# Two graph convolutions: 72 of 104 edge groups gathered from DRAM and 32 read from the table on the chip, in place of 59 and 45

## The reference, cut to what matters

```
msgs = embedding_weight[row] * norm[:, None]          # layer 1
out  = jax.ops.segment_sum(msgs, col, num_segments=n)

h    = features * norm_src[:, None]                   # layer 2
agg  = jax.ops.segment_sum(h[src], dst, num_segments=N_NODES) * norm_dst[:, None]
out  = relu(agg @ weight + bias)
```

## Time and profile before

| | us |
|---|---|
| median of 3 runs (lowest, highest) | 7875.66 (7863.07, 7904.74) |
| the profiled execution's own time | 7890.42 |
| its span | 7888.7 |
| PE busy in the span | 6027.0 (76%) |
| DVE busy | 3734.3 (47%) |
| POOL busy | 3873.9 (49%) |
| ACT busy | 1754.8 (22%) |
| L900, reading the table, PE busy | 1120.3 |
| L398, gathers of the convolutions, POOL busy | 458.7 and 443.0 (two groups of buffers) |

### The profile page before, as it was taken

How to read it: one execution, slowest core, us unless ns; L and a number is a source line. 1 busy time by engine, 2 the same in 40 slices (tenths; PEclk the granted TensorE clock), 3 DMA queues, 4 the chain that set the end, 5 groups by cost and what they waited for, 6 DMA issues and landing times.

```text
span 7888.7 us, 136475 instructions
## 1 busy us (share of the span) xinstructions
PE 6027.0 (76%) x46669; PEld 3955.1 (50%) x46669; DVE 3734.3 (47%) x7123; ACT 1754.8 (22%) x3748; POOL 3873.9 (49%) x4028
## 2 busy tenths in 40 slices
PE   5888887666666777677788886778878857778787
PEld 4666665566655666534444443344444424444444
DVE  5444443555564555534444445444444544444446
ACT  2222222333330000022222221222222222222221
POOL 4555553444435455355555542555555345555551
PEclk8888886777886777788888887888888879888888
DMA  4444442222212222233333332333333323333332
GB/s 102 129 129 131 128 128 85 53 56 56 57 49 63 62 62 59 57 74 90 88 91 91 91 86 57 84 89 90 88 88 92 87 54 89 88 90 89 93 87 64
DMA packets 689768, 660.52 MB, mean 84 GB/s; under 512 B 398899, under 2 KB 481274, under 8 KB 689082
## 3 DMA queue, kind: packets, MB, share of 16 engines
q1 hardware_dynamic: 555754, 484.41, 20.5%
q0 software_dynamic: 128960, 166.69, 11.1%
q10 hardware_dynamic: 4368, 0.70, 0.1%
HBM read 562.14 MB, written 89.17 MB: 83 GB/s over the span
## 4 chain that ended last, share of the span: by engine, by line
PE 49%; issue 20%; another core or an unknown queue 18%; DVE 7%; ACT 3%; DVEq 2%; DMA 0%; ACTq 0%; POOL 0%; SPq 0%; POOLq 0%
PE ps L1055 14%; PE ps L900 12%; PE ps L994 6%; PE ps L915 2%; PE ps L855 2%; PE ps L1005 2%; PE ps L1015 2%; PE ps L980 1%; PE ps L864 1%; PE ps L974 1%; DVE region L1778 1%; DVE acc L1803 1%; PE ps L842 1%; PE ps L1029 1%
## 5 line engine op out<-in xcount | busy, mean ns | idle before, releaser
L381 POOL DMA_INDIRECT rows<-table,idx x2340 | 2262.4, 967 | 2235.3 <-ACT region L651 1002.6
L1055 PE MATMUL ps<-region,hot 128*128 128x272 f32 x4992 | 1530.4, 458 | 282.6 <-DVE region L1756 149.3
L1055 PEld LDWEIGHTS ps<-region,hot 128*128 128x128 f32 x4992 | 1041.7, 219 | 677.6 <-issue 445.3
L900 PE MATMUL ps<-hot,region 128*128 128x192 bf16 (+1 forms) x8640 | 1120.3, 291 | 322.4 <-issue 291.3
L1803 DVE TENSOR_TENSOR acc<-acc,ps 128x272 f32 x1248 | 545.0, 437 | 1704.9 <-remote 804.5
L662 ACT ACTIVATE region<-ps 128x512 f32<-128x512 f32 x1248 | 677.6, 595 | 2707.6 <-remote 1428.2
L900 PEld LDWEIGHTS ps<-hot,region 128*128 128x128 bf16 x8640 | 911.2, 116 | 467.0 <-issue 391.3
L368 POOL DMA_INDIRECT rows<-table,idx x728 | 700.5, 962 | 530.0 <-PE ps L835 315.8
L994 PE MATMUL ps<-xT,wcat 64*128 64x512 f32 x2496 | 773.6, 697 | 179.3 <-ACT region L662 81.1
L1778 DVE TENSOR_TENSOR region<-ps,region 128x1056 f32<-128x1056 f32 x582 | 725.1, 1252 | 44.5 <-issue 40.9
L398 POOL DMA_INDIRECT rows<-table,idx x480 | 458.7, 956 | 506.6 <-PE ps L927 344.5
(11 more groups left out here) (304 smaller groups left out, 6836.1 us busy)
## 6 DMA issues: line engine op xcount, KB each, us to landing
hot<-hot_dram SPq DMA_DIRECT2D x624, 256.0 KB
turned<-turned_dram SPq DMA_DIRECT2D x624, 128.0 KB
rows<-table,idx POOLq DMA_INDIRECT x3548
hot_dram<-hot SPq DMA_DIRECT2D x104, 512.0 KB
region<-hot_dram SPq DMA_DIRECT2D x90, 512.0 KB
xwin<-table SPq DMA_DIRECT2D x1664, 24.0 KB
region<-d_dram SPq DMA_DIRECT2D x104, 256.0 KB
turned_dram<-turned SPq DMA_DIRECT2D x104, 256.0 KB
```

What stands on the lines that cost most here:

```text
L381: pool.indirect_dma_start(rows[:, n % 2, j, :], None, table, bass.IndirectOffsetOnAxis(ap=idx[:, s:s + 1], axis=0)).then_inc(rows_in3[n % ...
L900: mm = pe.matmul(ps[:, GB + i % 2, 224 * j:224 * j + n], bt[b][:, k, at:at + P], tabparts[:, k::FOLD, (2 + s) * C:(3 + s) * C], start=(k = ...
L1055: mm = pe.matmul(ps[:, sum_bank(k, side, i), 0:PC + H], hot[:, b, 4 * side + 2 * i + j, :], px[b][:, 4 * side + 2 * i + j, :], start=(j == ...
```

## The change

The bound in the rule that splits the groups goes from 9 to 11, and so `PLAIN` has 72 groups, `DENSE` 32 and `ITEMS` 128 dense items with 72 plain groups between them: two dense items and a plain group mostly (56 times), one dense item and a plain group 16 times. Nothing else is edited; all loops follow the lists, in both convolutions.

```
-DENSE = [g for g in range(G) if 7 * g % 16 >= 9]
-PLAIN = [g for g in range(G) if 7 * g % 16 < 9]
+DENSE = [g for g in range(G) if 7 * g % 16 >= 11]
+PLAIN = [g for g in range(G) if 7 * g % 16 < 11]
```

## The result

The changed kernel takes 7795.53 us in the median of four runs (7772.58 to 7798.94), the kernel before 7877.76 in the same session (7863.07 to 7904.74). The ratio is 0.990 with an interval of 0.988 to 0.992: faster by 1%. Predicted were 7821 us and a range of 7690 to 7970.

The account below looks back on a forecast made before the run. No engine is full; a hold on PE during POOL's gather runs sets the round. First convolution -41 us, second -13, together -54: 7890.42 to 7836 profiled, which is 15 above the median, so 7821 us; range 7690 to 7970.

Parts of the forecast that it names:

- The hold: Convolution rounds: from about a run's sixth gather until 1.6 us after its last, PE hardly gets on; signals arrive at 11.6.
- The rival without a hold: Convolutions: a round is its longest engine, POOL's 10.0 us, say 10.2; 7543 us; chance 0.1 together with the instruction-count rival.
- the one by PE's instruction count: Convolutions: PE gets no more than 12.1 to 12.7 instructions a us; -437 us, 7438 us; 0.1 together with the no-hold rival.
- Floor of 11.8 us: Convolution rounds: the plain sum's signal reaches POOL at 11.6 us, POOL starts at 11.8, pausing 1.8 us instead of 5.4.
- All hidden: Rival, both convolutions: everything hides in the hold, rounds of 11.8 us; -46 and -121 us, 7709 us; chance 0.2.
- Second convolution, 12.3 us a round: Second convolution's rounds at 12.3 us, bounds 11.8 and 13.1; 918 us before, 905 after, -13 us.
- the joined pair: With one dense item between plain groups (16 of 72 times), two gather runs join: 24.3 us for two rounds.
- the slip: Convolution rounds: at the lower clock a reading takes longer, the sum can slide into the hold; 0.5 us added.
- First convolution, 13.0 us a round: First convolution's rounds at 13.0 us, bounds 11.8 and 15.2; 995 us before, 954 after, -41 us.
- an extra of 0.7 us for the degree count: First convolution: 23 instructions more a round for the degree count; surcharge between 0 and 1.8 us, taken as 0.7.
- Joined throughout: Rival at the wait on `plain_summed`: gather runs join everywhere, rounds 13.1 and 15.2 us, 8022 us; throughout or mostly, chance 0.25.
- The ends: Each convolution's time from the last run's start: 35 us in the second, 37 in the first.

Follow-up runs that it names:

- E1: Changed kernel with one gather of eight per plain group after the first four groups, both convolutions, PE waiting for that one: 6968.24 us, ratio 0.883.
- e2: Changed kernel with the second convolution's gathers replaced by plain loads of the same size, started by ACT: 7393.34 us.
- e4: Kernel before, POOL waiting for its gathers to land after the fourth and eighth of each group in both convolutions: 7528.99 us, ratio 0.955.
- E3: Changed kernel, POOL waiting after each group's eighth gather until it has landed, both convolutions: 7768.2 us, ratio 0.986 to the kernel before.
- E5: Changed kernel with three plain groups made dense again (69 plain, 35 dense), no pauses: 7600.03 us, ratio 0.982 to the kernel before.
- e9: Kernel before with 53 plain and 51 dense groups, landing waits after gathers four and eight in convolutions, four in attention: 7155.63 us, ratio 0.908.
- E12: Changed kernel (72 plain, 32 dense) with landing waits after the fourth and eighth gather in the convolutions: 7843.64 us, ratio 0.9965 to the kernel before.

## Why the prediction was right, and where it was off

**The hold sets the round: held, and shown.** E1 takes the gathers away and the holes and late signals go; e2 keeps the bytes and they go; e4 keeps gathers and bytes, breaks the run at four, and most of the holes go, while the signals' lateness shrinks. The rival without a hold (7543 us) and the one by PE's instruction count (7438) are off by the result itself; the latter also by e4, where PE runs 7.0 to 8.1 matmuls in a us in the convolutions, for the 6.1 and 6.4 of the earlier trace rows.

**Floor of 11.8 us: held.** 37 single rounds at 11.94 us and 15 at 11.82, each with a sum that was done 3 to 8 us before POOL heard of it (at 7.1 to 8.8 in the second convolution; about 6.4 was predicted). In all 52 the semaphore moves 11.5 to 11.8 us after the run's start. The prediction has this for signals "in the second half of the run"; the semaphores show it to begin earlier. In the second convolution of the kernel before, signals sent 2 to 5 us after a run's start are already 0.7 to 1.5 us late in the median, and those sent at 5 to 7 us 5 to 6. "All hidden" (11.8 everywhere, 7709 us) failed on the other rounds.

**Second convolution, 12.3 us a round: too low by 0.27.** The step that failed is the joined pair, priced at 24.3 us and measured at 26.46. I had the hold end 1.6 us after the last gather, as after runs of eight, at 21.6 us, and the next sum 2.7 us later. PE is whole again at 22.7 (2713.37 - 2690.63) and the next run starts 3.7 us after that. A longer run holds longer. The 0.5 us that I had added for the slip wasn't there in single rounds (11.89 to 12.02 us). The fifth group joined the first four as well, so that both convolutions start with 40 gathers and not 32, and it took 19.9 us. Against 12.3 us a round the 14 pairs bring 14 x 1.86 = +26 us, the fifth group +8, the 37 single rounds -13 and the last group, joined to the one before, -2: 67 x 0.27 = +18. With the end +3 and the start -6 (40 us to the fifth group, for 46) 905 became 920, and the gain of 13 became nothing. E3 agrees with 25 us for the joining.

**First convolution, 13.0 us a round: too high by 0.51.** I carried an extra of 0.7 us for the degree count on top of 12.3. Two things differ from the second. In 51 rounds the sum lies in the hold, behind the count's matmuls, which costs that sum's own 0.7 us above the floor, 12.54. And the early sums are done at 3.5 to 5.1 us instead of 3.0 to 3.85, none of their signals gets through before 11.5, so that nothing joins after the start, and these 15 rounds stayed at 11.82. The sum's time can't be the whole reason: two of them are done at 3.53 and 3.70, and in the second convolution one done at 3.85 gets through. In the first, signals of the count (L935) sent only 0.5 to 1.3 us after a run's start are already 5.3 to 7.5 us late. What makes the hold begin earlier there is open. The 16 joinings that I had assumed for both convolutions did not happen here. 67 x 0.51 is -34 us, start and end -8: 954 became 911.5, and the gain of 41 became 88.

**The sum.** The errors, +15 and -42, go against each other; -54 was predicted, -87 came. That the total came as near as it did is partly luck, though each is inside its own bounds (12.57 in 11.8 to 13.1, 12.49 in 11.8 to 15.2).

**Joined throughout (8022 us): place right, size wrong.** It needed the signal to get through in every round. In the second convolution it gets through where the sum is done by 3.85 us after the run's start, in 14 of 51 runs, and not where it is done at 7.1 or later; none lies between. E5, without those early sums, has none.

**Signs.** Runs of eight with starts 11.7 to 13 us apart and some of sixteen: seen. The mask 11.6 us after a run's first gather: 2728.65 - 2717.09 = 11.56. POOL's idle time before L398 is 2.7 us a round in both, beside the 0.3 between gathers: seen. The ends, 35 and 37 us predicted, are 34.7 and 37.7. PE's busy time fell by 266 us, not 350. The prediction made no term of it; a matmul of L900 costs more in the new kernel, 306 ns for 293, at a granted clock of 0.70 for 0.74, and more of the trickle counts as busy.

The Trainium skill ("SBUF — State Buffer", section "Who interferes with whom") says that a DMA never contends with a compute engine. For e2's plain loads, 100 GB/s beside a PE without holes, the trace agrees. For runs of more than about five indirect gathers started by POOL e1 and e4 go against it, whatever the shared thing is; within the reading of the page that is no contention for SBUF, and none of these runs says where it sits.

**Open.** What in the chip holds PE and its signals: that the transfers are indirect, that their rows are scattered, or that POOL makes their descriptors; no run here parts them. Plain loads started by POOL, and indirect ones of consecutive rows, would. The recording of the profile isn't it, since e4's executions that were only timed (7514.71 to 7548.51 us) lie around the profiled one (7531.37), as those of the kernel before do. Also open is why breaking the runs gains nothing in the edge network, where PE's signals are late too.

## What to carry to other kernels

Where an engine has holes that "wait for nothing" and another engine's finished work is heard of late, look at what a third engine does in just these stretches; here it was a run of more than five gathers without a pause. Breaking such a run by waiting for the fourth gather's landing cost POOL 1.75 us of idling each time in place of 0.3 and gave the kernel 4.5%, with the attention 7.9%, and with the split made anew 9.2%; it is to be tried stage by stage, since the edge network lost by it. A split tuned while such a hold stands is tuned to the hold: with the pauses in, 72 plain groups lose to 59 and 59 to 53. So put the remedy in first, then choose the split.

## What the runs showed of the hardware

POOL starts an indirect gather of 128 rows every 1.25 us (0.94 busy, 0.30 between), and such a run, once past about five, lets PE start one or two matmuls at a time, with holes between. The starts stand on a grid of about 0.71 us: in the long run above they are at 2701.37, 2702.79 and 2703.51, then

```profile
2705.62 0.32 PE L900 MATMUL ps<-hot,region 128*128 128x192 bf16 x1 [1.78 <-issue]
...
2707.03 0.32 PE L900 MATMUL ps<-hot,region 128*128 128x192 bf16 x1 [1.09 <-issue]
...
2709.14 0.35 PE L900 MATMUL ps<-hot,region 128*128 128x224 bf16 x1 [1.79 <-issue]
```

so 0.72, 1.41 or 2.11 us apart, one, two or three steps. In the first convolution's trickle through L935 it is 0.71 as well. Of all 760 pairs of neighbouring PE matmuls in the changed kernel's two convolutions that start 0.5 to 3 us apart, 498 lie within 0.05 us of one, two, three or four such steps.

PE's signals are late from earlier in a run than its instructions. In the second convolution sums done 3.0 to 3.85 us after a run's start moved the semaphore 0.4 to 4.0 us later; those done at 3.5 to 5.1 us in the first moved it at 11.5 to 11.6, though PE keeps full pace until about 7 us. Even in e4's runs of four they are up to 3.4 us late; with single gathers (e1) or plain loads (e2) they are not late at all.

The hold lasts longer after a longer run: 1.8 us past the last gather's end after eight (1710.50 to 1712.3), 3.1 after sixteen (2710.30 to 2713.37). With 0.6 us after every fourth gather the rounds are shorter (14.37 us for 15.33 in the second convolution, in a batch whose kernel before is 1.7% faster). With 1.75 us PE's reading has no holes, and the late signals are fewer and less late.

The granted clock goes down with the holes. It is 0.70 to 0.78 in the convolutions with them, a mixture of the levels of 1.2 and 2.4 GHz, and 0.92 to 0.97 in e1, e2 and e9, where PE's long holes are gone. E12 has the pauses too, but its rounds last as long as POOL's gathers and waits, and PE, with less work in a round, idles; it stays at 0.73.
